# A two-layer kernel (attention, then a chunked scan) with the scan's preparation spread into the scan and the last gelus moved

## The reference, cut to what matters

```python
# layer 0, for each of the two axes (64 sequences of 64 tokens)
q, k, v = rope(ln(a) @ Wq), rope(ln(a) @ Wk), ln(a) @ Wv
out_axis = elu(softmax(q @ k.T) @ v @ Wo + bo)
x = x + (out_i + out_j) / 2
# layer 1
u = layernorm(x)                                   # 32 sequences of 128 tokens
z, xBC, dt = split(u @ in_proj_w.T)
xc = silu(causal_conv4(xBC)); xs, B, C = split(xc)
dt = softplus(dt + dt_bias); A = -exp(A_log)
h_t = h_{t-1} * exp(dt_t * A) + (dt_t * xs_t) B_t;  y_t = h_t . C_t + D * xs_t
y = y * silu(z); y = y * rsqrt(mean(y**2) + eps) * norm_w @ out_proj_w.T
x = x + wn_linear(y)
return x + fc2(gelu(fc1(layernorm(x))))
```

## Time and profile before

| | us |
|---|---|
| median of 3 runs (310.57 to 311.52) | 310.67 |
| the profiled execution | 309.12 |
| its span in the trace | 307.3 |
| busy PE / DVE / ACT / POOL | 239.4 / 204.6 / 166.6 / 115.1 |
| mean granted clock of TensorE | 0.901 |

### The profile page before, as it was taken

The page is one execution under the profiler, slowest core; times in us unless marked ns, Lnnn a source line. Parts: engine busy times, 40 slices in busy tenths (PEclk is TensorE's granted clock), DMA queues, the critical chain, the costliest instruction groups (busy, mean ns, idle before and its releaser), DMA issues.

```text
span 307.3 us, 8733 instructions
## 1 busy us (share of the span) xinstructions
PE 239.4 (78%) x3666; PEld 148.7 (48%) x3666; DVE 204.6 (67%) x335; ACT 166.6 (54%) x289; POOL 115.1 (37%) x94
## 2 busy tenths in 40 slices
PE   8963878985979768658568799979999948956653
PEld 3642555663757445527564456524544424434421
DVE  2798667879398646353725968997867785484323
ACT  2255466766377683544248644673558328723291
POOL 1613194375234600004001975483968742300000
PEclk9998599999699999596977999997999979997768
DMA  6923021100111100043144000000000000011003
GB/s 179 327 31 105 34 70 45 63 36 36 36 36 55 54 2 5 1 101 69 33 99 101 0 2 2 2 3 0 5 2 0 2 0 2 2 34 36 1 0 68
DMA packets 25222, 12.96 MB, mean 42 GB/s; under 512 B 22240, under 2 KB 22496, under 8 KB 25056
## 3 DMA queue, kind: packets, MB, share of 16 engines
q1 hardware_dynamic: 23456, 11.24, 13.7%
q10 hardware_dynamic: 1728, 1.17, 1.5%
HBM read 4.63 MB, written 1.05 MB: 18 GB/s over the span
## 4 chain that ended last, share of the span: by engine, by line
PE 42%; DVE 30%; ACT 14%; issue 12%; DVEq 0%; ACTq 0%
PE ring L575 20%; PE score L575 8%; PE p_turn L575 6%; PE oz L575 4%; DVE s_cen L1134 4%; DVE rot_cos L1075 3%; PE ring L580 2%; DVE rot_sin L1079 2%; DVE mix L1224 2%; DVE ln_s L910 2%; DVE ln_v L930 2%; DVE xhat L945 2%; ACT prob_t L1375 2%; DVE cen L918 2%; ACT ln_l L936 1%
## 5 line engine op out<-in xcount | busy, mean ns | idle before, releaser
L1595 POOL TENSOR_TENSOR a_msk<-dt_fin,c_sb 128x512 f32<-128x512 f32 x32 | 40.0, 1249 | 33.6 <-DVE dt_fin L1051 23.8
L1224 DVE TENSOR_TENSOR mix<-dec,g_m 128x512 f32<-128x512 f32 x32 | 31.4, 987 | 2.2 <-ACT dec L1461 1.5
L1122 DVE TENSOR_REDUCE s_max<-score 128x16 f32<-128x1024 f32 x16 | 19.6, 1222 | 14.6 <-PE score L575 14.5
L1375 ACT ACTIVATE prob_t<-p_turn 128x512 f32<-128x512 f32 x32 | 17.6, 594 | 15.5 <-PE p_turn L580 15.0
L1580 POOL TENSOR_TENSOR dtx<-xv,dt_fin 64x512 f32<-64x512 f32 x16 | 19.8, 1238 | 13.2 <-PE p_turn L575 12.2
L925 ACT ACTIVATE sqr<-cen 128x512 f32<-128x512 f32 (+1 forms) x13 | 7.7, 595 | 31.0 <-DVE cen L918 31.0
L575 PEld LDWEIGHTS p_turn<-mix,dtx 128*32 128x32 f32 x512 | 11.0, 110 | 27.5 <-issue 14.7
L575 PE MATMUL score<-a_msk,c_sb 128*128 128x512 f32 x44 | 24.3, 635 | 0.0
L954 POOL TENSOR_TENSOR k_rot<-rot_cos,rot_swap 128x512 f32<-128x512 f32 x7 | 8.9, 1275 | 35.3 <-DMA rot_swap<-rot_sin 35.3
L1385 ACT ACTIVATE prob<-s_cen 128x1024 f32<-128x1024 f32 x16 | 16.8, 1053 | 9.5 <-DVE s_cen L1134 9.5
L575 PE MATMUL oz<-prob_t,v_bd 128*32 128x64 f32 x512 | 11.3, 234 | 12.4 <-ACT prob_t L1375 9.3
(11 more groups left out here) (185 smaller groups left out, 579.7 us busy)
## 6 DMA issues: line engine op xcount, KB each, us to landing
rot_swap<-rot_sin SPq DMA_DIRECT2D x28, 128.0 KB, 2.1
p_sb<-params SPq DMA_DIRECT2D x1, 1520.0 KB, 10.9
x_tok<-x SPq DMA_DIRECT2D x16, 64.0 KB, 4.0
ut_a<-u SPq DMA_DIRECT2D x8, 126.0 KB, 2.6
ut_b<-u SPq DMA_DIRECT2D x8, 124.0 KB, 2.5
ut_b<-u SPq DMA_DIRECT2D x8, 122.0 KB, 2.5
out<-x_tok SPq DMA_DIRECT2D x10, 64.0 KB, 2.2
back<-x ACTq DMA_DIRECT2D x4, 128.0 KB, 6.5
```

What stands on the lines that cost most here:

```text
L1122: v.tensor_reduce(s_max[:, n % 2, :], sc, AX, ALU.max).then_inc(s_maxed, 1)
L1224: v.tensor_tensor(mix[:, e % LAPS, :, :], dec[:, e % LAPS, :, :], wide(g_m[:, e // 4 % 2, e % 4, :], SSM_H), ALU.mult)\
L1375: a.activation(prob_t[:, e % 2, 4 * hp:4 * hp + 4, :].rearrange("p k n -> p (k n)"), PT[hp], ACT.Identity)\
L1595: gp.tensor_tensor(a_msk[:, m % LAPS, :, :], deep(dt_fin[:, 0, SSM_H * m:SSM_H * (m + 1)], GRID), wide(cst("tri"), SSM_H), ALU.mult).then_ ...
```

## The change

The attention has 19 steps now. `xt`, `ut` and `xp` stand in slot a. The chunks' `xt` come at steps 13, 15, 17 and at scan step 3, `ut` at 15, 17 and at scan steps 0 and 5. The first four `xp` (chunk 0) come at step 17, the other twelve at scan steps 0 to 11. The softplus is made in three parts, of 8, 8 and 16 tiles: at steps 17 and 18, at scan steps 4 to 6, and at scan steps 12 to 14, and POOL asks for the second part at step 7 and for the third at step 15. `wo` of chunks 4 to 7 stand at steps 12, 14, 16, 18 instead of 13, 15, 17, 18. z0 and z1 of a chunk come two scan steps later (for chunk 3: 22 and 23 instead of 20 and 21), and so do the Tanh (`x_tanh`) and product (`x_silu`) of the later quarters of xv. For groups 2 and 3 of the tail f1, f2, fo come one step later or stay, and ht stands ahead of f1 within a step. The tiles in SBUF are laid out anew so that the scan's early tiles don't lie on those of the attention still in use.

```diff
-ATT_STEPS = 25
+ATT_STEPS = 19
-XT_STEP = (14, 16, 18, 19)
-UT_STEP = (16, 18, 20, 21)
-XP_STEP = (18, 18, 19, 19, 20, 20, 21, 21)
+WO_STEP = (5, 7, 9, 11, 12, 14, 16, 18)
+XT_STEP = (13, 15, 17, ATT_STEPS + 3)
+UT_STEP = (15, 17, ATT_STEPS, ATT_STEPS + 5)
+XP_STEP = (17,) * 4 + tuple(range(ATT_STEPS, ATT_STEPS + 12))
...
-        c += [("ut", q) for q in range(CHUNKS) if UT_STEP[q] == n]
-        c += [("xt", q) for q in range(CHUNKS) if XT_STEP[q] == n]
-        c += [("xp", k) for k, at in enumerate(XP_STEP) if at == n]
+        a += [("wo", k) for k in range(ATT_CHUNKS) if WO_STEP[k] == n]
+        a += [("ut", q) for q in range(CHUNKS) if UT_STEP[q] == n]
+        a += [("xp", k) for k, at in enumerate(XP_STEP) if at == n]
+        a += [("xt", q) for q in range(CHUNKS) if XT_STEP[q] == n]
...
-MLP_STEPS = ((28, 29, 30), (28, 30, 31), (36, 37, 38), (37, 38, 39), (38, 39, 40))
+MLP_STEPS = ((28, 29, 30), (28, 30, 31), (37, 38, 39), (38, 39, 40), (38, 39, 40))
-SOFTPLUS_STEP = 8
-DT_STEP = 22
-DT_PARTS = ((0, 2 * len(XP_STEP)), (2 * len(XP_STEP), TILES))
+DT_PARTS = ((0, CT), (CT, 2 * CT), (2 * CT, TILES))
+LOG_STEP = (ATT_STEPS + 4, ATT_STEPS + 12)
+DT_STEP = ((17, 18, 18), (ATT_STEPS + 4, ATT_STEPS + 5, ATT_STEPS + 6), (ATT_STEPS + 12, ATT_STEPS + 13, ATT_STEPS + 14))
...
-        steps[CT * (c - 1) + 4].append(("z0", c))
-        steps[CT * (c - 1) + 5].append(("z1", c))
+        steps[CT * (c - 1) + 6].append(("z0", c))
+        steps[CT * (c - 1) + 7].append(("z1", c))
...
+        steps[NORM_STEP[o]].append(("ht", o))
+    for o in range(len(GROUPS)):
         for kind, at in zip(("f1", "f2", "fo"), MLP_STEPS[o]):
             steps[at].append((kind, o))
-        steps[NORM_STEP[o]].append(("ht", o))
...
 # ScalarE
-                a.preload_act_table_set("natural_log_exp_and_others")
                 a.wait_ge(dt_chain, 6 * part + 1)
...
+                if n >= ATT_STEPS and n in LOG_STEP:
+                    a.preload_act_table_set("natural_log_exp_and_others")
...
 # GpSimd
-                    if m == DT_PARTS[1][0] - 1:
-                        gp.wait_ge(dt_ready, 4)
+                    for part in range(1, len(DT_PARTS)):
+                        if m == DT_PARTS[part][0] - 1:
+                            gp.wait_ge(dt_ready, 2 * part + 2)
```

More of the change, by code:

```diff
@@ L118, in ssm_uses @@
     steps = {m: [] for m in range(SSM_STEPS)}
-    for m in range(TILES // 2 - len(XP_STEP)):
-        steps[m].append(("xp", len(XP_STEP) + m))
+    for m in steps:
+        for kind, at in (("xt", XT_STEP), ("ut", UT_STEP), ("xp", XP_STEP)):
+            steps[m] += [(kind, k) for k, n in enumerate(at) if n == ATT_STEPS + m]
     for c in range(1, CHUNKS):
         steps[CT * (c - 1) + 2].append(("bc", c))
-        steps[CT * (c - 1) + 4].append(("z0", c))
-        steps[CT * (c - 1) + 5].append(("z1", c))
+        steps[CT * (c - 1) + 6].append(("z0", c))
+        steps[CT * (c - 1) + 7].append(("z1", c))
     for o in range(len(GROUPS)):
@@ L267, in build @@
         c_s = sb("c_s", [2 * STATE, 2, CW], ssm)
-        z_s = sb("z_s", [P, 2, 2, CT, GRID], ssm)
+        dt_fin = sb("dt_fin", [P, 2, TILES * SSM_H], ssm)
         a_msk = sb("a_msk", [P, LAPS, SSM_H, GRID], ssm)
@@ L279, in build @@
         xv = sb("xv", [P, TILES, INNER], ssm)
-        dt_fin = sb("dt_fin", [P, 2, TILES * SSM_H], ssm)
         ssm.close()
@@ L1106, in att_use, with step_end @@
                     last.then_inc(w_out_ready, 1)
+            def step_end(n):
+                for q in range(CHUNKS):
+                    if n == XT_STEP[q] + 1:
+                        ln_vector_b(v, CHUNKS + q)
+                    if n == UT_STEP[q] - 1:
+                        ln_vector_c(v, CHUNKS + q)
+                for part in range(len(DT_PARTS)):
+                    for stage, at in zip((softplus_a, softplus_b, softplus_c), DT_STEP[part]):
+                        if n == at:
+                            stage(part)
             for use in att_steps[-1]:
@@ L1149, in _ @@
                     ln_vector_c(v, 3)
-                g, odd = divmod(n, 2)
-                c = g - 2
-                if (0 <= c < ATT_CHUNKS - 1) if odd else c == ATT_CHUNKS - 1:
+                if n in WO_STEP:
+                    c = WO_STEP.index(n)
                     v.wait_ge(wo_biased, c + 1)
@@ L1165, in _ @@
                     late_scales()
-                for q in range(CHUNKS):
-                    if n == XT_STEP[q] + 1:
-                        ln_vector_b(v, CHUNKS + q)
-                    if n == UT_STEP[q] - 1:
-                        ln_vector_c(v, CHUNKS + q)
-                if n == XT_STEP[0] + 1:
+                if n == XT_STEP[0] + 2:
                     filled(v, ("v", ATT_CHUNKS - 1))
@@ L1353, in softplus_b, with step_end @@
                 a.activation(dt_tmp[:, 4, cols_of], dt_tmp[:, 2, cols_of], ACT.Exp, scale=-1.0).then_inc(dt_act, 1)
+            def step_end(n):
+                for q in range(CHUNKS):
+                    if n == XT_STEP[q]:
+                        ln_scalar_a(a, CHUNKS + q)
+                if n >= ATT_STEPS and n in LOG_STEP:
+                    a.preload_act_table_set("natural_log_exp_and_others")
+                for q in range(CHUNKS):
+                    if n == XT_STEP[q] + 1:
+                        ln_scalar_b(a, CHUNKS + q)
+                for part in range(len(DT_PARTS)):
+                    for stage, at in zip((softplus_a, softplus_b), DT_STEP[part]):
+                        if n == at:
+                            stage(part)
             def k_masks(g):
@@ L1405, in _ @@
                     late_weights()
-                if n == DT_STEP:
-                    softplus_a(0)
-                if n == DT_STEP + 1:
-                    softplus_b(0)
-                for q in range(CHUNKS):
-                    if n == XT_STEP[q]:
-                        ln_scalar_a(a, CHUNKS + q)
-                    if n == XT_STEP[q] + 1:
-                        ln_scalar_b(a, CHUNKS + q)
+                step_end(n)
             def bc_use(c):
@@ L1467, in _ @@
                         z_use(use)
+                    elif kind == "ut":
+                        att_use(use)
                     elif kind == "ms":
```

54 lines of the change are left out of this document (22 added, 32 removed).

## The result

The changed kernel takes 319.6 us (median of 4 runs, 315.7 to 320.9) against 310.6 (4 runs, 306.5 to 311.5): 9.0 us slower. Executions of one kernel fall into a fast and a slow state; the medians here are of all of them, and the ratios with an interval are of the fast ones alone, here 1.039 with a 95% interval of 1.032 to 1.047, some 12 us. The profiled execution took 320.86 us with a span of 319.1, 11.8 us above the span of before.

What follows compares the result with a forecast made beforehand. Chains and a slow clock bound the stretch before the scan, PE its first third (DVE right behind), chains steps 23 to 28. -15 + 7.2 + 5 + 1.5 + 6.3 - 1.2 = +3.8 gave 314.5 us; range 304.0 to 323.0.

Steps and rivals of the forecast that it cites:

- Part 1: Start of the scan: first a_msk at 152.5 instead of 167.44, since it needs only chunk 0; -15 us (-17.5 to -11).
- part 4: First scan steps: PE, without work for about 8 us before, runs at the lower clock; +1.5 us (0 to 3).
- Part 2: PE work moved behind the first decay sum (four xp, xt(3), two ut) has its full price; +7.2 us (+5 if idle time absorbs it).
- 4 x 1.01, 2.1 and 2 x 0.5: PE time in the scan for four more xp, xt(3) and two ut; together +7.2 us.
- Part 3: Two gates in the scan where POOL's a_msk(7) and a_msk(15) wait for dt's softplus; +5 us (0 to +8).
- 4.4 each: Cost of each dt gate: chain 3.7 to 5.1, clock 1.6 more, less what POOL and PE catch up.
- Less the old 3.5: Credit for the kernel before's single dt gate with its waits and slow clock, taken off the two new gates; 3.5 us.
- Part 5: Scan steps 23 to 28: z1 of chunk 3's Tanh behind a preload makes seven table loads; +6.3 us (+3.8 to +8).
- Part 6: End of the kernel: three of four table loads go, last addition at 302.4 to 303.1 instead of 303.56; -1.2 us (-2.5 to 0).
- the scan absorbs the gates: Rival: in the scan a_msk come before PE asks, so gate and start-clock costs vanish; 306.5 us, chance 0.25.
- DVE becomes the bound of the scan: Rival: DVE gets about 6 us more in the scan and cannot take it; 5 to 9 above forecast, 321 us, chance 0.20.
- The parts cancel: Rival: start at 150 and gates of 2 each give -2.7; at 151.5 within 0.9 of no change; chance 0.13.

Runs made afterwards that it cites:

- e6: Kernel after with one more table preload, the scan's softplus pieces one step earlier and ut of chunk 3 at scan step 6 instead of 5; 301.8 us.
- e9: Kernel after with only the softplus pieces inside the scan one step earlier, table loads unchanged; 312.1 us, ratio 1.010 to the kernel before.
- e5: Kernel after with one more table preload and the softplus pieces inside the scan one step earlier; 303.3 us, ratio 0.980 to the kernel before.
- e11: Kernel before with only z0 and z1 of chunk 3 two scan steps later; 315.5 us, ratio 1.035 to the kernel before.
- e1: Kernel after with the common Ln and Exp table preloaded at the second ms too; 313.0 us, ratio 1.018 to the kernel before.
- e7: Kernel before with only the new tail (f1, f2, fo of groups 2 and 3, ht ahead of them); 309.7 us, ratio 1.002.
- e3: Kernel after with no dt gates: every tile reads the first part's dt, leaving the dt of tiles 8 to 31 out; 316.2 us.
- e2: Kernel after with the softplus's last piece written ahead of xp and z at scan steps 6 and 14; 314.2 us, ratio 1.029 to the kernel before.
- e12: Kernel after with the four xp of chunk 1 put back ahead of the scan; 323.2 us, ratio 1.048 to the kernel before.

## Why the prediction was right, point by point

The direction and the range held; the size was off: +3.8 was forecast and +9.0 came (+11.8 between the two profiled executions, which is past the forecast's own +1 to +9). That the range up to 323.0 held the result is in part luck: its upper end was set by the rival of DVE as the bound, which did not happen. By the steps of the prediction:

- **Part 1** (-15) and **part 4** (+1.5) were right, part 1 in its path too (ut(1) at 134.51, the end of xt(2) at 142.36, then 9.2 us): the first a_msk came 15.9 earlier, the first decay sum 14.7, and the low clock that part 4 expected stands there (2.08 and 1.92 for z and the decay sum instead of 1.02 each, 2.0 in all).
- **Part 2** (+7.2) was right as work: e6 has 7.19 us more of PE in the stretch (that it agrees to a hundredth is luck, since the clocks were 0.99 and 0.98). What the step "4 x 1.01, 2.1 and 2 x 0.5" left out was that a moved ut brings its wait along. xt(3) at step 3 and ut(3) at step 5 leave the layer norm two steps: PE waited 1.75 us, and e6 gives 1.76 back.
- **Part 3** was the term that was mis-sized, while the chain up to the gated decay sum was right in each of its links. "4.4 each", 8.8 for both, was forecast; at the two gates e9 gets back 7.0 and 6.0, and 11.5 over the stretch, with 1.9 us of waits still there. The waits themselves were forecast to 3.7 to 5.1 and measured 4.15 and 4.79 (the 2 to 4 that the prediction gave as a sign to look for did not fit its own sum). The step that failed is "with the clock behind it 1.6 more, less what POOL and PE catch up at once: 4.4 each": 4.4 is the middle of the waits alone, so what was to be caught up took the whole clock term away. In the trace PE runs at half the clock for the next five us, 6.29 for what takes 3.41 in e5, and nothing is caught up. From the balance: the stretch got 5.8 us of PE's busy time that is no work (12.99 less 7.19).
- "Less the old 3.5" was a credit that does not show: with the gates mended (e6), PE's idle time in the stretch, 4.69, is about the 5.05 of the kernel before. Where the old wait went, others stand (1.06 and 0.83 for a_msk).
- Together parts 2 to 4 between tiles 0 and 25 were 20.05, where 12.2 to 13.7 had been forecast.
- **Part 5** (+6.3) was right: +6.7 in the kernel after, +7.1 in e11, and -4.7 for the five loads of e1. The Trainium skill (ScalarE: Activation LUTs, What ACT_TABLE_LOAD costs) gives a drain of some 1380 ns beside each load; the sum by that figure was not what happened: L952's load starts at 257.49, 0.02 us behind the end of the Ln before it (257.17 + 0.30), and its Exp at 258.78, 1.29 us behind the load's start, so that there is no drain on either side.
- **Part 6** (-1.2) is small and not settled. The last addition of the kernel after stands 1.3 nearer to the last decay sum, but from there to the end it takes 1.1 more, where the stores of two groups come together, which the step that stopped at the last addition did not count; and in e7 the same tail is worth nothing that can be told. Three loads less on ACT were not three loads less on the path.

Of the rivals, "the scan absorbs the gates" is refuted by the waits of 4.15 and 4.79. "DVE becomes the bound of the scan" is refuted for the kernel as a whole, by its own test too: between the first decay sum and the twelfth step (154.64 to 205.10) DVE is idle for 18.7 us, and PE waits for mix once, for 0.56. DVE is busy for 59.90 of 94.48 in the stretch, less than the 62.56 of 74.43 before, though about 6 more was forecast and it has 21 instructions more. The same 109 instructions take 63.16 in e6, where POOL does not stand at a gate for so long, so 3.3 us of DVE's time hang on POOL; why the 21 instructions add no more than 0.6 even there is not shown. But a part of the rival is true, as e3 shows: with the gates gone and the softplus in place, PE waits for mix. The Trainium skill (SBUF — State Buffer, SBUF: two separate sides) has it that DVE and POOL share one pair of ports, which one of them holds for a whole instruction while the other waits. The pieces of the softplus agree: they take 0.22 us each (64 columns) or 0.29 (128) beside an idle POOL and took 1.10 in the earlier trace rows.

"The parts cancel" did not happen either, and its sum was slightly off: two gates of 2 less the old 3.5 make 0.5 and not 1, and a start at 151.5 gives -1.2 by its own terms, not a value within 0.9 of no change.

## What to carry to other kernels

When work that prepares data is spread into a pipeline that is full, its instructions have their full price (7.2 us forecast, 7.19 found), and their waits and the low clock behind them come on top (13 us here), so place each piece one step ahead of where the last consumer's order would let it stand, not just in front of it. The pieces of the softplus one step earlier, one preload more and ut(3) one step later are three edits of a line each, and turn 319.6 into 301.8, 7.4 under the kernel before that ran beside it (309.2). And look at where a function of another table lands when an activation is moved: one Tanh behind a preload made seven loads.

## What was not expected of the hardware

A wait of PE can cost more than its length, and how much more is not fixed by the length. Measured at the two gates as the excess over e9 (which has no wait at the first and one of 1.05 at the second), from decay sum 6 to 8 and from 14 to 16: a wait of 1.60 us cost 1.7, one of 2.77 cost 4.0 (both e2), one of 4.15 cost 7.0 and one of 4.79 cost 6.0 (both in the kernel after). Behind the wait of 4.15 PE took 6.29 us from this decay sum to the next, and 3.41 for the same instructions in e5 (179.47 to 182.88). But nearly equal waits at the same place ended differently:

```profile
171.78 1.09 PE L594 MATMUL ring<-c_sb,xhat 128*128 128x128 f32 x4 [1.75 <-DVE xhat L959]
...
182.33 2.07 PE L589 MATMUL score<-a_msk,c_sb 128*128 128x512 f32 x2 [4.01 <-POOL a_msk L1612]
```

These two are of e1. Behind 4.01 us its low clock lasted some 3 us (the next decay sum came 4.9 behind); behind 1.75 us ahead of ut of chunk 3 the clock was low at once (1.09), while in the kernel after the same transposes behind the same wait took 0.63. In e12 a decay sum behind a wait of 4.01 took only 1.12, and the rows behind it ran slow. What decides it is open here.

DVE's busy time depends on what POOL does: DVE was busy for 62.56 us in 74.43 of the scan before and for 59.90 in 94.48 after, with 21 instructions more, and the same 109 instructions took 63.16 in e6. A DVE operation beside an idle POOL is shorter (0.29 against 1.10 us). A busy share of 0.84 was in part the other engine's doing.
